# A state-space scan with interleaved matmuls: the state's sum and the piece change places on TensorE

## The reference

```python
xi, z = split(x @ W_in.T)                 # 512 channels each
u  = silu(conv4(xi) + conv_b)
dt = softplus(dbl[..., :16] @ W_dt.T + b_dt)     # dbl = u @ W_xproj.T
def step(h, inp):                          # over the 1024 tokens
    dA = exp(dt_t[:, :, None] * A)
    h = h * dA + (dt_t * u_t)[:, :, None] * B_t[:, None, :]
    return h, einsum('bcs,bs->bc', h, C_t)
y = (ys + u * D_skip) * silu(z);  s = y @ W_out.T
```

## Time and profile before

| | us |
|---|---|
| median of three runs | 2197.11 |
| the profiled execution | 2187.27 |
| its span | 2185.5 |
| TensorE busy (matmul) | 1866.1 |
| VectorE busy | 1669.4 |
| ScalarE busy | 1263.6 |
| GpSimd busy | 1214.6 |

### The profile page before, as it was taken

The page is one execution under the profiler, slowest core; times in us unless marked ns, Lnnn a source line. Parts: engine busy times, 40 slices in busy tenths (PEclk is TensorE's granted clock), DMA queues, the critical chain, the costliest instruction groups (busy, mean ns, idle before and its releaser), DMA issues. The chain is left out here.

```text
span 2185.5 us, 26582 instructions
## 1 busy us (share of the span) xinstructions
PE 1866.1 (85%) x8596; PEld 1058.5 (48%) x8596; DVE 1669.4 (76%) x2189; ACT 1263.6 (58%) x1685; POOL 1214.6 (56%) x651
## 2 busy tenths in 40 slices
PE   6689988997998898789879888998886677998996
PEld 3345545654654463233334332533342235887885
DVE  4975797397579525899999999999989995332787
ACT  4764874586486515666654665466544434655774
POOL 2601810360181002789988999888976674222676
PEclk9899999999999999899999999999988999999998
DMA  7420641344064216899898888988899984223453
GB/s 203 97 59 6 148 99 58 106 95 109 15 140 97 78 35 44 288 312 286 280 319 300 285 286 295 306 290 275 296 298 368 331 327 140 97 96 101 140 160 105
DMA packets 177321, 402.68 MB, mean 184 GB/s; under 512 B 48174, under 2 KB 77104, under 8 KB 176034
## 3 DMA queue, kind: packets, MB, share of 16 engines
q1 hardware_dynamic: 165154, 371.09, 54.9%
q0 software_dynamic: 12032, 29.90, 4.8%
HBM read 356.30 MB, written 45.51 MB: 184 GB/s over the span
## 5 line engine op out<-in xcount | busy, mean ns | idle before, releaser
L1336 POOL TENSOR_TENSOR late<-late,rows 128x1024 f32<-128x1024 f32 x256 | 602.5, 2361 | 144.8 <-DVE late L1816 141.6
L1987 PE MATMUL m_Q<-late,ident_m 128*128 128x512 f32 x1024 | 524.4, 644 | 152.8 <-POOL late L1336 119.3
L1816 DVE TENSOR_TENSOR_SCAN late<-m_Q,late 128x1024 f32<-128x1024 f32 x256 | 586.2, 2290 | 44.9 <-ACT m_Q L1522 16.4
L1522 ACT ACTIVATE m_Q<-late,acol 128x1024 f32<-128x1024 f32 x256 | 286.1, 1118 | 368.4 <-DVE late L1816 366.7
L1987 PEld LDWEIGHTS m_Q<-late,ident_m 128*128 128x128 f32 x1024 | 193.7, 201 | 449.6 <-POOL late L1336 253.2
L1809 DVE TENSOR_TENSOR late<-m_Q,rows 128x1024 f32<-128x1024 f32 x256 | 306.9, 1199 | 9.9 <-DMA rows<-bc_s 9.8
L553 DVE SCALAR_TENSOR_TENSOR early<-early,work 128x1024 f32<-128x1024 f32 x128 | 155.9, 1218 | 43.7 <-ACT early L699 41.7
L2050 PE MATMUL m_Q<-late 128*128 128x128 f32 x1248 | 158.8, 281 | 9.0 <-issue 1.3
L2050 PEld LDWEIGHTS m_Q<-late 128*128 128x128 f32 x1248 | 147.0, 193 | 36.3 <-issue 35.0
L709 ACT ACTIVATE early<-early 128x1024 f32<-128x1024 f32 x128 | 135.2, 1056 | 26.9 <-DVE early L558 25.8
L710 ACT ACTIVATE early<-early,halfpi 128x1024 f32<-128x1024 f32 x128 | 145.7, 1138 | 0.0
(11 more groups left out here) (243 smaller groups left out, 3340.9 us busy)
## 6 DMA issues: line engine op xcount, KB each, us to landing
rows<-bc_s SPq DMA_DIRECT2D x512, 512.0 KB, 5.7
rows<-st_s SPq DMA_DIRECT2D x64, 384.0 KB, 5.8
r_s<-late SPq DMA_DIRECT2D x39, 256.0 KB, 2.0
rows<-st_s SPq DMA_DIRECT2D x64, 128.0 KB, 6.4
st_s<-early SPq DMA_DIRECT2D x8, 768.0 KB, 5.3
xin<-in_x SPq DMA_DIRECT2D x4, 1024.0 KB, 5.6
xres<-in_x SPq DMA_DIRECT2D x4, 1024.0 KB, 5.5
mx_s<-s SPq DMA_DIRECT2D x4, 1024.0 KB, 4.5
```

Source lines behind the costliest of these rows:

```text
L1336: nc.gpsimd.tensor_tensor(pr[:, n % NH, :], h[:, n % NH, :], cb[:, n % NCB, :], ALU.mult).then_inc(pr_ok, 1)
L1522: A(dA[:, :], dt[:, (b * KI + m) % 2, :], ACT.Exp, scale=acol[:, m, i % NS:i % NS + 1]).then_inc(dA_ok, 1)
L1816: v_.tensor_tensor_scan(h[:, n % NH, :], dA[:, :], dB[:, n % 2, :], 0.0, ALU.mult, ALU.add).then_inc(h_ok, 1)
L1987: ins = mm(half(Y, c), ident[:, :], half(pr[:, n % NH, :], c), start=False, stop=(n % NS == NS - 1), skip_group_check=True)
```

## The change

In each step of the scan stage TensorE issues the state (or the three states of step 3) first and the prologue's piece after them, where before the piece came first. Everything else, on TensorE and on the other engines, stays as it is.

```diff
                         job = filler(b, m, s)
-                        if job:
-                            half_job(*job)
                         if s == 3:
                             add_state(n - 3)
                             add_state(n - 2)
                         if n and s not in (1, 2):
                             add_state(n - 1)
+                        if job:
+                            half_job(*job)
```

## The result

The changed kernel took 2285.12 us (median of 4, 2282.0 to 2288.07), the kernel before 2198.12 us in the same series: ratio 1.0404, 95% interval 1.0376 to 1.0432. It is 4% slower, where 2261 us was predicted, with a range of 2218 to 2290. A second series of the changed kernel gave 2276.41 us against 2196.7 (ratio 1.0362, 1.0332 to 1.0392). The part of the program ahead of the scan stage varies by some 15 us between profiled executions of all the kernels here (the first scan began at 895.4 and 885.9 us in the two of the changed kernel, at 880.7 us before), and no instruction of it was changed. So I read the scan stage by itself, from the start of the first scan to the end of the last. It repeats closely: 1028.0 and 1027.7 us in the two profiled executions of the changed kernel; before it was 943.4 us, in one. The stage is 84.6 us longer, and the prediction had 64.

The account below looks back on a forecast made before the run. VectorE was taken to bound the scan stage, paying for each late decay. Late scans of 70.6 us plus 8.5 of clock, less 12.4 of old waits and 2.9 of row load, gave +64: 2261 us, range 2218 to 2290.

Parts of the forecast that it names:

- The bound and the chain: Scan stage: VectorE bounds; product, state, piece, ScalarE's evacuation and decay follow in turn, so a late piece delays the scan.
- late = L + e + r - 0.94: Scan's lateness in us, if above zero: GpSimd's product lag L, evacuation e, ScalarE's link behind it r, margin 0.94.
- Step 8 of tile 0: Scan after step 7's output piece, whose evacuation has a softplus behind it: 0.8 us late.
- Step 12 of tile 0 in batches 1 and 2: Scan after the piece behind rate and drive: 4.9 and 6.1 us late, 1.7 of each for the clock.
- The last burst of tile 2 in batch 1: Step 15, after rate and drive at 12 and a DMA, with a link: 4.4 us late.
- How much F moves: Piece F(n) of step n comes a whole step (3.53 us) later, not just a state's length (1.82 us).
- The row load of batch 0: VectorE's wait of 2.85 us for a row load gets more time and goes: -2.9 us.
- Step 3: States 0, 1 and 2 pass ahead of the piece; 0.8 us late at step 4 of tile 1.
- The clock: TensorE's slow clock after five long waits with a piece behind adds 1.7 us each, 8.5 us.
- Rival 3: Larger: clock falls at all 13 bursts and a slow state delays the next evacuation; +90, 2287 us, chance 0.17.
- No change: Rival 4: ScalarE's evacuations have slack enough; 2197 us, chance 0.05.
- the second rival: Faster: state first cures states late behind pieces, and with them GpSimd's products and gates; -13, 2184 us, chance 0.05.

Follow-up runs that it names:

- the first experiment: Against the changed kernel, ScalarE does its prologue work (evacuations and links) one step later; 2211.93 us, ratio 1.0073 to the kernel before.
- The third experiment: Against the changed kernel, GpSimd makes drive of the next tile in step 11 in place of step 8 of tile 0; 2263.38 us.
- the kernel with softplus ahead: Against the changed kernel, ScalarE's softplus link goes ahead of the evacuation where it stood behind it; 2271.59 us.
- the extra matmuls: Against the changed kernel, TensorE does six extra matmuls at step 10 of tile 0 ahead of its wait for the late product; 2276.46 us.
- the mended kernel of before: Against the kernel before (piece first), the next input load goes behind step 14's rows and drive to step 11 of tile 0; 2192.47 us.

## Why the prediction was right, and where it was short

**The bound and the chain.** Right. VectorE pays for each late decay; scan, product and decay kept their mean durations to 0.01 us; ScalarE's waits for pieces are the cause (the first experiment) and come from a wait for a product one step later. The chance of 0.89 for slower rested on this. The marks of the prediction came, most of them larger than named: 102.5 us of waits for the decay (about 80 named), ScalarE's wait behind rate and drive of 6.79 us (up to 5). One came the other way: VectorE's waits for row loads, which were to fall, rose from 9.8 to 14.7 us.

**The formula late = L + e + r - 0.94.** Right where TensorE's clock is up. Step 8 of tile 0, 0.8 expected: 0.70 (4.23 - 3.53). Steps 13 and 15 of tile 1 in batch 1, 5.5 expected: 0.8 + 4.5 = 5.3. Tile 2 up to step 8 in batch 1, 3.1 expected: 0.96 + 2.19 = 3.15. Where half clock fell on the burst, its 1.7 has to be added. Step 12 of tile 0 in batches 1 and 2, 4.9 and 6.1 expected: 4.9 and 6.1. The last burst of tile 2 in batch 1 was put at 4.4 without the clock; it took half clock (the state 3.59 us), 4.4 + 1.7 = 6.1, and the scan was 6.05 late. The third experiment took the lag away and most of the late scan went.

**How much F moves.** I took the whole step against the length of a state (+23 in all). Right: the late scans above came out as the whole step gives. Outside the bursts the state goes on waiting for its product (91 waits of TensorE, 141.8 us, 76 and 119.3 before).

**The sum.** 64 predicted, 84.6 measured. Three terms were mis-sized:

- *The row load of batch 0*, put at -2.9 us ("that gets more time"). I saw a wait for rows and took it for one that slack heals. It was SyncE's wait for piece 10, which the change makes later. VectorE waited 10.5 us there; mending it gave 7.2 us of the stage back. That is the one place where the prediction had no mechanism at all: it did not ask what SyncE's list waits for.
- *Step 3*, put at 2 to 3 us. Its piece was what filled TensorE's wait for the skip term. Alone it costs 10.1 us, and leaving it out of the change gives 14.2: some 7 to 12 more than my term.
- *The clock*, put at 5 x 1.7 = 8.5 us, for the bursts where before's trace showed it. The mean granted clock fell from 0.95 to 0.92 of full speed in the stage, and steps with no burst have it, too: step 8 of tile 1 in batch 1 took 5.81 us where the formula gives 4.3 (the state ahead of its piece took 3.58), step 11 of tile 2 5.60. The reading under the term, that only the longest waits pay, was already wrong in the trace of before:

```profile
1289.25 1.98 PE L1987 MATMUL m_Q<-late,ident_m 128*128 128x512 f32 x4 [2.68 <-POOL late L1336]
...
1458.42 3.67 PE L1987 MATMUL m_Q<-late,ident_m 128*128 128x512 f32 x4 [2.16 <-POOL late L1336]
```

  Rival 3 had named a clock that falls more often, and its 2287 us came out nearest to 2285; but its mechanism (half clock at all bursts) is only part of the excess, and one large burst, at steps 13 to 15 of tile 1 in batch 1, ran at full speed (its state took 1.99 us). How the 13 us beside the load divide between step 3 and the clock elsewhere is not separated: half clock falls on the states of step 3, too (7.08 us for the twelve instructions).

The Trainium skill, page "TensorE: Matmul & The Clock Gate", section "HAM oscillation — how this bites in real kernels", says that when TensorE waits long for data between its groups the clock falls and the next group starts slow, each time again. This case agrees in part: half clock comes behind such waits (2.48 and 3.13 us for state and piece behind 3.34 us), but not each time, and the last pause does not decide by itself. Behind the same 3.34 us in the kernel with softplus ahead they took 1.99 and 1.89 us, and before, a state took 3.67 us behind 2.16 us and 1.98 behind 2.68.

**No change, faster.** Both fell. GpSimd's product, which was to gain by an early state, waits 15.9 us for TensorE now, 1.2 before. The -13 us of the second rival also counted the 1.1 us of the two gates twice, as they stand in its 12.4 already.

## What to carry to other kernels

In an in-order queue, ask of an instruction that is moved behind a wait not only what it waits for but who reads its result, in which step, and what that reader has queued behind it; the price is there (64 of 85 us here went when the reader was shifted and the moved piece stayed where it was). List every queue that waits for the moved piece, the DMA queue's too: a single load that waits for it holds all loads behind it. And a piece that seems mere filler may be what fills another wait: at step 3 its place was worth 10 to 14 us.

## What the runs showed of the hardware that I had not expected

Two executions of one program place half clock on almost the same steps (stages 1028.0 and 1027.7 us), yet an edit can move it to other steps, and the length of the pause does not tell where it falls: with two identical orders of TensorE's instructions, the state and piece behind a pause of 3.34 us took 2.48 and 3.13 us in the changed kernel and 1.99 and 1.89 in the one with softplus ahead. Mends of 1 to 2 us each were therefore partly or wholly paid back elsewhere (the extra matmuls, the links, and the mended kernel of before).
